# A new order of work in the token-mixing phase, and an opening with one semaphore per weight

## The reference

```python
x = x + attn(layernorm(x)); x = x + moe(layernorm(x))
# attn: xx = shift(x) - x;  xk = x + xx*maa_k  (v, r, g alike)
#  r, k, v = xr@Wr.T, xk@Wk.T, xv@Wv.T (per head);  g = gelu(xg@Wg.T)
#  per chunk: att = rc @ kc;  yc = att*Wmat @ vc + rc @ state * wb
#             state = ws*state + kc*wk @ vc
#  y normalised per head, * ln_w + ln_b;  out = (yn*g) @ Wo.T
# moe: probs = softmax(x@gate_w.T), top 2, slot = running count per expert, dropped over capacity
#  expert: (silu(d@w1) * (d@w3)) @ w2, weighted by probs and added
```

## Time and profile before

| | |
|---|---|
| median of 3 runs | 914.38 us (911.5 to 915.5) |
| profiled execution | 918.7 us, span 917.0 |
| mean granted TensorE clock | 0.989 |
| busy, share of the span | TensorE 93%, ScalarE 54%, VectorE 50%, GpSimd 50% |
| waits of TensorE, 0 to 45 us | 22.3 us in five waits |
| waits of TensorE, 45 to 345 us | 15.7 us in 23 waits |

### The profile page before, as it was taken

The page is one execution under the profiler, slowest core; times in us unless marked ns, Lnnn a source line. Parts: engine busy times, 40 slices in busy tenths (PEclk is TensorE's granted clock), DMA queues, the critical chain, the costliest instruction groups (busy, mean ns, idle before and its releaser), DMA issues. The chain is left out here.

```text
span 917.0 us, 18900 instructions
## 1 busy us (share of the span) xinstructions
PE 848.2 (93%) x6791; PEld 706.8 (77%) x6792; DVE 460.4 (50%) x1174; ACT 490.7 (54%) x875; POOL 462.2 (50%) x497
## 2 busy tenths in 40 slices
PE   2899999999999999897999999999799999999995
PEld 1667777777677777787889789879689879889885
DVE  5767777777777766333442342442242443352330
ACT  2578777777788768253443453443353344353331
POOL 4534666677765756456237345237237136447024
PEclk9999999999999999899999999999999999999998
DMA  4572121112211122447025327025225214414013
GB/s 150 223 277 65 49 88 49 49 60 67 81 37 37 37 67 77 158 120 174 1 81 87 112 64 133 3 81 88 72 81 88 71 41 109 90 41 48 13 18 40
DMA packets 50464, 73.94 MB, mean 81 GB/s; under 512 B 5056, under 2 KB 42176, under 8 KB 50368
## 3 DMA queue, kind: packets, MB, share of 16 engines
q1 hardware_dynamic: 35488, 53.46, 17.6%
q0 software_dynamic: 14592, 19.18, 12.3%
q10 hardware_dynamic: 288, 0.01, 0.0%
HBM read 38.41 MB, written 34.22 MB: 79 GB/s over the span
## 5 line engine op out<-in xcount | busy, mean ns | idle before, releaser
L1547 POOL TENSOR_TENSOR wlo<-wraw,whi 128x448 fp32r<-128x448 f32 x84 | 102.6, 1225 | 209.9 <-ACT whi L1604 209.9
L1824 PE MATMUL p<-xh,whi 128*128 128x512 f32 (+1 forms) x504 | 190.9, 379 | 12.8 <-DVE xl L1723 4.9
L1826 PE MATMUL p<-xh,wlo 128*128 128x512 f32 (+1 forms) x504 | 190.4, 378 | 0.0
L1825 PE MATMUL p<-xl,whi 128*128 128x512 f32 (+1 forms) x504 | 189.6, 376 | 0.0
L1741 DVE TENSOR_TENSOR hid<-gated,p 128x512 f32<-128x512 f32 (+1 forms) x126 | 81.1, 643 | 211.6 <-ACT gated L1618 211.6
L1555 POOL DMA_INDIRECT out<-ysb,index x80 | 125.4, 1568 | 91.2 <-ACT ysb L1640 57.3
L1618 ACT ACTIVATE gated<-p 128x512 f32<-128x512 f32 (+1 forms) x126 | 71.0, 563 | 186.3 <-PE p L1826 186.3
L1844 PE MATMUL py<-whi,hh 128*128 128x256 f32 x469 | 135.2, 288 | 6.6 <-DVE hl L1043 3.5
L1846 PE MATMUL py<-whi,hl 128*128 128x256 f32 x469 | 132.6, 283 | 0.0
L1845 PE MATMUL py<-wlo,hh 128*128 128x256 f32 x469 | 132.5, 283 | 0.0
L1824 PEld LDWEIGHTS p<-xh,whi 128*128 128x128 f32 x504 | 95.1, 189 | 33.3 <-issue 11.3
(11 more groups left out here) (195 smaller groups left out, 1417.7 us busy)
## 6 DMA issues: line engine op xcount, KB each, us to landing
wraw<-in_w SPq DMA_DIRECT2D x24, 896.0 KB
disp<-wraw SPq DMA_DIRECT2D x16, 662.5 KB, 8.9
xtok<-disp SPq DMA_DIRECT2D x16, 530.0 KB, 5.1
x_ring<-in_x SPq DMA_DIRECT2D x16, 256.0 KB, 3.0
out<-x SPq DMA_DIRECT2D x16, 256.0 KB
xtok<-disp SPq DMA_DIRECT2D x8, 265.0 KB, 6.0
out<-ysb,index POOLq DMA_INDIRECT x80
disp<-row,slot_i POOLq DMA_INDIRECT x64
```

The costliest lines, as they stand in the source:

```text
L1547: nc.gpsimd.tensor_tensor(wlo[e.const % 2][m][:, cut], wraw[k][:, cut], whi[e.const % 2][m][:, cut].bitcast(F32), ALU.subtract).then_inc(w ...
L1824: nc.tensor.matmul(dst[:, 0:w], hi[m][:, wcut], xh[xcut], start=(kt == 0), stop=False)
L1825: nc.tensor.matmul(dst[:, 0:w], hi[m][:, wcut], xl[xcut], start=False, stop=False)
L1826: ins = nc.tensor.matmul(dst[:, 0:w], lo[m][:, wcut], xh[xcut], start=False, stop=(kt == KT - 1))
```

## The change

pX's release is split: `group_log` holds the logarithm and signals `grlog_ready`, `group_rstd` holds the exponential, and `turn1` waits for the former. `const_in` becomes `maa_in` and `proj_in[0..3]`. In the opening the decay tables' exponents and the parity move behind the first two mixings, `center_v` behind the third, and ScalarE's `pairs` ahead of `receptance`; the sums of `set_dve` that are waited for follow that order. All five queues get a new order, in the loop and in the tail: TensorE has `across`, `outer` and the first `within` right behind `scores_a`, then `turn1` and `project_g`; `project_o` and `logits` stand ahead of `turn_k`; on GpSimd `weight_low` stands ahead of `mixed_g`, and the last piece of it at the very end. Most of what looks moved in the loops is a rotation: the end of one round became the start of the next. `stats1` and `norm1` run one step less ahead.

```diff
--- before.py
+++ after.py
@@ -367,3 +367,4 @@
     x_in = [sem(f"x_in{k}") for k in range(RING)]
-    const_in, late_in, decay_in = sem("const_in"), sem("late_in"), sem("decay_in")
+    maa_in, late_in, decay_in = sem("maa_in"), sem("late_in"), sem("decay_in")
+    proj_in = [sem(f"proj_in{k}") for k in range(4)]
     set_dve, set_pool, set_act = sem("set_dve"), sem("set_pool"), sem("set_act")
@@ -382,3 +383,3 @@
     ysq_ready, ssum_done, yn_ready = sem("ysq_ready"), sem("ssum_done"), sem("yn_ready")
-    y_ready, grstd_ready = sem("y_ready"), sem("grstd_ready")
+    y_ready, grlog_ready, grstd_ready = sem("y_ready"), sem("grlog_ready"), sem("grstd_ready")
     z_ready, zg_ready, wo_done = sem("z_ready"), sem("zg_ready"), sem("wo_done")
@@ -389,3 +390,3 @@
     count_done, slot_ready, sent = sem("count_done"), sem("slot_ready"), [sem(f"sent{k}") for k in range(2)]
-    dve_chain, pool_chain, act_chain = sem("dve_chain"), sem("pool_chain"), sem("act_chain")
+    dve_chain, pool_chain = sem("dve_chain"), sem("pool_chain")
     taken_ready = sem("taken_ready")
@@ -399,3 +400,3 @@
 
-    NCONST, NLATE = 1 + 4, 1 + 4
+    NLATE = 1 + 4
     SENT = 16 * TPS * 2
@@ -429,5 +430,5 @@
         load_x(0)
-        sp.dma_start(maa_sb[:], maa).then_inc(const_in, 16)
+        sp.dma_start(maa_sb[:], maa).then_inc(maa_in, 16)
         for k in range(4):
-            sp.dma_start(w_in_sb[k], weights[k].rearrange("(k p) c -> p k c", p=P)).then_inc(const_in, 16)
+            sp.dma_start(w_in_sb[k], weights[k].rearrange("(k p) c -> p k c", p=P)).then_inc(proj_in[k], 16)
         load_x(1)
@@ -538,2 +539,4 @@
                 pool.wait_ge(diff_ready, b + 1)
+                if b == 0:
+                    pool.wait_ge(maa_in, 16)
                 wait(pool, proj_done[3], b)
@@ -579,7 +582,7 @@
 
-        for c in range(-3, TAIL):
+        for c in range(-2, TAIL):
             scatter(c - 4)
             norm2(c - 2)
-            norm1(c + 3)
-            if c == -3:
+            norm1(c + 2)
+            if c == -2:
                 tables()
@@ -587,2 +590,3 @@
             decayed_r(c + 1)
+            weight_low(c - 6)
             mixed_g(c + 1)
@@ -590,3 +594,2 @@
                 empty_rows()
-            weight_low(c - 6)
             chain.reset()
@@ -596,4 +599,4 @@
         norm2(13)
+        weight_low(10)
         gated(14)
-        weight_low(10)
         scatter(12)
@@ -601,2 +604,3 @@
         norm2(14)
+        weight_low(9)
         gated(15)
@@ -605,12 +609,10 @@
         norm2(15)
-        weight_low(11)
         scatter(14)
         chain.reset()
-        early_index()
         scatter(15)
         chain.reset()
-        weight_low(9)
+        early_index()
+        weight_low(11)
 
     def on_scalar(act):
-        chain = Chain(act, act_chain)
         for dst, src in ((lam_row, decay_row), (lam_ch, decay_ch)):
@@ -649,3 +651,3 @@
                 if b == 0:
-                    act.wait_ge(set_dve, 3)
+                    act.wait_ge(set_dve, 2)
                 wait(act, att_done, TPS * b)
@@ -710,3 +712,3 @@
 
-        def group_rstd(b):
+        def group_log(b):
             if 0 <= b < STEPS:
@@ -716,3 +718,7 @@
                 wait(act, yn_ready, b)
-                chain.link(nc.scalar.activation(grstd[:], pX[:], ACT.Ln, scale=1.0 / N, bias=gn_eps[:, 0:1]))
+                nc.scalar.activation(grstd[:], pX[:], ACT.Ln, scale=1.0 / N, bias=gn_eps[:, 0:1]).then_inc(grlog_ready, 1)
+
+        def group_rstd(b):
+            if 0 <= b < STEPS:
+                act.wait_ge(grlog_ready, b + 1)
                 nc.scalar.activation(grstd[:], grstd[:], ACT.Exp, scale=-0.5).then_inc(grstd_ready, 1)
@@ -770,4 +776,8 @@
         for c in range(-2, TAIL):
+            logit_exp(c - 3)
+            weight_high(c - 4)
+            value(c)
+            group_log(c - 1)
+            group_rstd(c - 1)
             turned1(c + 1)
-            normed1(c + 2)
             column(c + 1)
@@ -776,3 +786,2 @@
             normed2(c - 2)
-            receptance(c + 1)
             if c == -1:
@@ -780,14 +789,16 @@
             pairs(c + 1)
+            receptance(c + 1)
             key(c + 1)
+            normed1(c + 2)
+            turned2(c - 2)
+            square_y(c)
             keep_y(c)
-            square_y(c)
-            turned2(c - 2)
-            logit_exp(c - 2)
-            value(c + 1)
-            group_rstd(c)
-            weight_high(c - 4)
-
+
+        logit_exp(12)
+        value(15)
+        group_log(14)
+        group_rstd(14)
+        normed2(13)
         scaled(14)
         gate(15)
-        normed2(13)
         turned2(13)
@@ -797,14 +808,16 @@
         early_hi(1)
+        group_log(15)
+        logit_exp(13)
         group_rstd(15)
-        logit_exp(13)
+        early_gate(0)
         normed2(14)
         scaled(15)
-        early_gate(0)
+        weight_high(11)
+        early_gate(1)
         turned2(14)
+        early_gate(2)
         early_hidden_hi(0)
-        early_gate(1)
-        weight_high(11)
+        logit_exp(14)
         early_hidden_hi(1)
-        logit_exp(14)
-        early_gate(2)
+        early_gate(3)
         normed2(15)
@@ -813,9 +826,8 @@
         logit_exp(15)
-        early_gate(3)
         early_gate(4)
         early_hidden_hi(3)
+        early_gate(5)
         early_hidden_hi(4)
-        early_gate(5)
+        early_hidden_hi(5)
         early_gate(6)
-        early_hidden_hi(5)
         early_hidden_hi(6)
@@ -843,3 +855,3 @@
 
-            dve.wait_ge(const_in, 16 * NCONST)
+            dve.wait_ge(proj_in[2], 16)
             wv4 = WV.rearrange("p k (h n) -> p (k h) n", n=N)
@@ -853,3 +865,3 @@
                                  axis=AX_X).then_inc(set_dve, 1)
-            dve.wait_ge(set_dve, 3)
+            dve.wait_ge(set_dve, 2)
 
@@ -895,3 +907,3 @@
                 if b == 0:
-                    dve.wait_ge(const_in, 16 * NCONST)
+                    dve.wait_ge(maa_in, 16)
                 for c in range(KT):
@@ -1045,19 +1057,3 @@
 
-        for c in range(-4, TAIL):
-            best_two(c - 3)
-            mask(c, 0, 0)
-            mask(c, 0, 1)
-            mask(c, 0, 2)
-            mask(c, 0, 3)
-            masked_kv(c)
-            if c == -1:
-                decay_logs()
-                center_v()
-                head_parity()
-            shifted(c + 1)
-            mixing(c + 1, 0)
-            normed_y(c - 1)
-            state_a(c)
-            tally(c - 3)
-            mixing(c + 1, 1)
+        for c in range(-3, TAIL):
             mask(c, 1, 0)
@@ -1066,4 +1062,11 @@
             mask(c, 1, 3)
+            state_b(c)
             mixing(c + 1, 2)
-            stats1(c + 4)
+            if c == -1:
+                center_v()
+            slots(c - 3)
+            stats1(c + 3)
+            residual(c - 1)
+            logit_max(c - 2)
+            stats2(c - 1)
             if c == -1:
@@ -1074,18 +1077,19 @@
                 slot_tables()
-            slots(c - 3)
-            logit_max(c - 2)
-            residual(c - 1)
-            stats2(c - 1)
-            state_b(c)
+            best_two(c - 2)
+            tally(c - 2)
+            mask(c + 1, 0, 0)
+            mask(c + 1, 0, 1)
+            mask(c + 1, 0, 2)
+            mask(c + 1, 0, 3)
+            masked_kv(c + 1)
+            state_a(c + 1)
+            shifted(c + 2)
+            mixing(c + 2, 0)
+            normed_y(c)
+            mixing(c + 2, 1)
+            if c == -2:
+                decay_logs()
+                head_parity()
             chain.reset()
 
-        best_two(12)
-        mask(15, 0, 0)
-        mask(15, 0, 1)
-        mask(15, 0, 2)
-        mask(15, 0, 3)
-        normed_y(14)
-        tally(12)
-        masked_kv(15)
-        state_a(15)
         mask(15, 1, 0)
@@ -1097,38 +1101,38 @@
         residual(14)
+        stats2(14)
         early_lo(0)
         early_lo(1)
-        stats2(14)
         logit_max(13)
-        normed_y(15)
         best_two(13)
         tally(13)
+        early_hidden(0)
+        normed_y(15)
         slots(13)
         chain.reset()
-        early_hidden(0)
+        early_hidden(1)
         residual(15)
+        stats2(15)
+        logit_max(14)
         early_hidden_lo(0)
-        early_hidden(1)
-        logit_max(14)
-        stats2(15)
+        early_hidden(2)
         best_two(14)
         tally(14)
-        early_hidden(2)
-        early_weight()
+        early_hidden_lo(1)
         slots(14)
         chain.reset()
-        early_hidden_lo(1)
+        early_weight()
+        early_hidden(3)
         logit_max(15)
-        state_b(15)
+        early_hidden_lo(2)
         best_two(15)
         tally(15)
-        early_hidden(3)
+        early_hidden(4)
         slots(15)
         chain.reset()
-        early_hidden_lo(2)
-        early_hidden(4)
         early_hidden_lo(3)
+        early_hidden(5)
+        state_b(15)
         early_hidden_lo(4)
-        early_hidden(5)
+        early_hidden_lo(5)
         early_hidden(6)
```

(52 more changed lines are left out.)

## The result

In the comparison made first, the changed kernel takes 890.9 us (890.3 to 893.9, 4 runs) against 914.9 (911.5 to 915.5, 4 runs): ratio 0.975, 95% interval 0.972 to 0.978. The forecast was 894. On two of the chips used for the experiments the same kernel is slower than the one before: 929.5 against 918.4 (ratio 1.012, 1.010 to 1.015) and 927.2 against 916.0 (1.011, 1.010 to 1.013). Each outcome repeats in all executions of its chip; the experiments are mostly about what divides the two.

The account below looks back on a forecast made before the run. TensorE, busy 93% of the span, was taken as the bound, so only its waits could go: 11.8 + 1.6 - 1.0 + 6.0 + 2.0 = 20.4 off 914.4 gives 894. The 8 in 10 range was 886 to 914.

Parts of the forecast that it names:

- Turn1: Phase one: TensorE's 14 waits at turn1 for ScalarE's grstd, 11.8 us, all go with release at the logarithm's end.
- the 2.66 us of the Trainium skill: ScalarE's table switch before the logarithm: at this cost turn1 still waits 0.8 in 14 steps, 905; chance 0.02.
- Masks: Phase one: scores_b's 6 waits for VectorE's masks, 3.1 us, fall away; 1.6 counted as present in timed runs.
- the pinch: First within of each step, wanted about when its mask is ready: 0.07 us a step charged, 1.0 over 14.
- The size of a step: Loop of phase one, from one scores_a to the next: about 19.4 us in place of 20.6.
- Opening: First project_r at 11.7 instead of 19.00, masks at 25.8, scores_b about 29.4; worth 6.0 us, ends 4.5 and 7.
- The end: End of phase one: last count 1.5 to 2.5 us earlier than the rest; worth 2.0, ends 0 and 4.
- The sign named for the wrong case: Profile after, end of phase one: a down projection that waits for `wlo`, GpSimd's weight split, would show the forecast wrong.
- late signals bite: Loop steps with scatters: masks start late, first within waits some 3.0 us a step; 13 slower, 927; chance 0.15.

Follow-up runs that it names:

- e1: Kernel before with only turn1's wait moved from the exponential to the logarithm, all orders old: 914.7 us against 918.4, ratio 0.997.
- e7: Kernel before with GpSimd's row scatter moved behind norm2, about 2 us later: 957.5 us against 918.4, ratio 1.044.
- e0: Changed kernel, unchanged, on another chip, with late signals: 929.5 us against 918.4 for the kernel before, ratio 1.012.
- e4: Changed kernel with TensorE's old order of the loop: 908.6 us beside the changed kernel's 929.5, ratio 0.990 to the kernel before.
- e8: Changed kernel with row scatters behind the norms, waiting for scores_b, third row and index buffers: 915.1 us beside 927.2, ratio 0.999 to the kernel before.

## Why the prediction was right, and where it wasn't

*Turn1.* Right in mechanism: 14 waits, 11.8 us, gone; the logarithm ended 0.54 ahead of turn1 (I had 0.6). Its size was short: I took the idle time in the brackets, which counts from the modelled end of project_g, 1.99 after its start, while the next group can start 1.83 after it. e1 shows 1.03 a step, 14.4 in 14 steps, not 11.8. The table load took 1.29 from its start to the logarithm here too (168.80, 170.09), so the 2.66 us of the Trainium skill (ScalarE: Activation LUTs, What ACT_TABLE_LOAD costs) don't show in the new place either.

*Masks.* No wait is left, where I charged 1.0 for the pinch. But what I said of the late masks failed, and with it the argument against the rival. It held that TensorE's other signals are used at once; in the same step of the kernel before project_g's is 0.5 late. "The late ones look like much of what the profiled run is longer by" took a property of the chip for one of the profiler. e7 and e0 show it in timed runs; the 4 us between the profiled execution and the median are about what the kernel before loses to it.

*The size of a step.* I had 19.4 us, it is 18.80. 20.56 held 1.13 idle, and 1.76 are gone, so 0.63 is missing in my sum. 0.34 of it is TensorE's order (e4 against the changed kernel): groups follow each other closer (project_v to sums 1.74 in place of 1.81; the projections above, 0.2 of it). Most of the rest is waits whose brackets read too short: 0.18 at turn1, and 0.07 at the mask, where within to scores_b took 0.71 in place of the 0.36 of a step without a wait, for 0.28 shown. This term, some 8 us over the ring, wasn't in the sum.

*Opening.* 6.0 forecast, 6.45 by turn_k(1) (36.90 against 43.35); project_r at 11.75, masks at 26.24, scores_b at 29.66, as reckoned.

*The end.* 2.0 forecast; from the last head sums (343.91 against 313.51) to the first down matmul (380.00 against 348.60) the changed kernel's lead grows by 1.0. That is two things: by the last of the early expert's matmuls it is 33.3 (376.14 against 342.85), mostly because the kernel before had the clock at 0.5 there, from 363.6 to 370.4, and the changed one didn't, and the wait ahead of down takes 1.9 back. The sign named for the wrong case came up: down waits 5.36 for `wlo` (before, 3.48 for `hl`), where VectorE's last half was ready at 346.3, 2.3 earlier. Behind it the granted clock is 0.5 from 347.5 to 354.4, half of full speed (1.2 against 2.4 GHz), and the down matmuls stand 0.21 apart, later 0.12. By the starts of the experts' down projections the lead, 31.4 us at 348.60, is 30.4 by the second, 27.8 by the third (between them the clock is 0.5 again, from 385.1 to 391.9, in the changed kernel alone) and 27.5 at the end. From profile to profile that is 11.8 + 3.1 + 6.5 + some 8.5 + 1.0 less 3.8, 27; from median to median 24.0, since the kernel before was profiled where signals are late and timed where they weren't. The missed spacing, the lost clock and this difference cancelled to a forecast 3 us off: that closeness is luck.

*The rival "late signals bite"* had 0.15, 927 and the right condition, a scatter 1.2 to 1.9 us ahead of the scores. It is what two chips of three show for the changed kernel, 927 and 929.5. Its mechanism was half right: the first within waits little (0.8 us in two waits). The delayed signals hold TensorE's own issue in the outer products, and the clock falls behind that.

Open: why a chip has late signals. In the steps compared no row of the two outcomes differs ahead of the delay, and the scatter stands 1.31 ahead of the scores in both. Nor is the window the whole condition: in e8 project_k's signal, given at +3.5, came on time, as did those of the expert work behind the last blocks' scatters. In the steps read, the first late signal was that of a group of small tiles (32 rows or 32 columns), and later ones seemed queued behind it. That was read from traces, not tried.

## What to carry to other kernels

Treat a GpSimd scatter as something that can delay TensorE's signals up to 6 us from its start, and put it, by a wait on a TensorE signal if need be, where the next readers have slack: the same order won 24 us on one chip and lost 11 on others, and the gate, with the last weight split moved too, made that 17 won on such a chip; the gate alone cost nothing on a chip without the lateness. Read what a wait costs from start to start against a step without it, not from the idle time in brackets (1.03 against 0.84 here). When a profiled execution is longer than the timed ones, look for what differs before calling it the profiler, and time on another chip. Release an accumulator at its last reader, not at the end of the chain that uses the value.

## Not expected of the hardware

- TensorE's signals behind four row scatters come 1.0 to 3.1 us late on some chips (e0), in 12 steps of 12, and with the same program on another never by more than 0.45.
- The same delay stops TensorE in the midst of 32 short matmuls that wait for nothing (0.46 us become 3.15), and the following clock stretch at 0.5, in every second step from the fourth on, makes eight matmuls of project_g take 3.27 us in place of 1.89.
- A full 128x128 group of eight takes 1.82 or 1.83 us to its successor with another full group ahead of it or behind it, 1.92 to 1.93 between two groups of small tiles.
